# A token mixer of two attentions and a router on Trainium2: the small jobs in another order, and two lists of row numbers for the scatters

## The reference

```python
h = layernorm(x) * (1 + ca) + sa
# linear attention, 16 heads of 16
qf, kf = elu(q) + 1, elu(k) + 1
out = (qf @ (kf.T @ v)) / (qf . sum(kf) + 1e-6)
x = x + ga * (out @ wo.T + bo)
h = layernorm(x) * (1 + cb) + sb
# softmax attention, 16 query heads of 16, 4 heads of keys and values
src = h + softmax(q @ k.T / 4) @ v @ ow + ob
src = rmsnorm(src) * norm1_w
# router: the two best of 8 experts a row; a capacity for each expert
probs = sigmoid(src @ gate_w); sel, w = top2(probs)
ranks = number of earlier rows of the same expert
padded[sel * capacity + ranks] = src        # if ranks < capacity
out = experts(padded) gathered, weighed and summed
x = x + gb * rmsnorm(src + out) * norm2_w
```

## Time and profile before

| | us |
|---|---|
| median of 3 runs | 3377.61 |
| lowest and highest | 3371.54 and 3377.68 |
| the profiled execution, its own time | 3384.39 |
| its span, first to last instruction | 3382.7 |
| the mixer's steps in it, first to last weighing (L3188) | 1366.4 to 2716.3 |

### The profile page before, as it was taken

The page is one execution under the profiler, slowest core; times in us unless marked ns, Lnnn a source line. Parts: engine busy times, 40 slices in busy tenths (PEclk is TensorE's granted clock), DMA queues, the critical chain, the costliest instruction groups (busy, mean ns, idle before and its releaser), DMA issues. The chain is left out here.

```text
span 3382.7 us, 58016 instructions
## 1 busy us (share of the span) xinstructions
PE 3135.4 (93%) x18353; PEld 1927.6 (57%) x18353; DVE 2082.6 (62%) x5622; ACT 1663.4 (49%) x3743; POOL 1118.9 (33%) x1508
## 2 busy tenths in 40 slices
PE   7899999999989976999999999999998859999997
PEld 3667767677665653344444444444443348888882
DVE  7777777777772233677777777777777632222226
ACT  3565565655641113666666666666665611111116
POOL 2132232322342123334444444444443322222224
PEclk9999999999999988999999999999999979999998
DMA  8110110101125841112222222222222137777758
GB/s 288 5 73 36 57 51 36 72 36 66 42 88 200 303 169 29 54 54 72 74 73 73 74 73 73 68 73 72 71 73 72 51 99 238 230 235 238 225 169 298
DMA packets 266210, 370.48 MB, mean 110 GB/s; under 512 B 41615, under 2 KB 201579, under 8 KB 263904
## 3 DMA queue, kind: packets, MB, share of 16 engines
q1 hardware_dynamic: 250592, 329.82, 30.2%
q0 software_dynamic: 14832, 34.57, 2.8%
q10 hardware_dynamic: 544, 3.15, 0.2%
HBM read 242.38 MB, written 130.39 MB: 110 GB/s over the span
## 5 line engine op out<-in xcount | busy, mean ns | idle before, releaser
L2425 ACT ACTIVATE pT<-psum 128x512 f32<-128x512 f32 x1024 | 599.1, 599 | 363.2 <-PE psum L3176 348.0
L2709 DVE TENSOR_REDUCE negmax<-psum 128x2 f32<-128x1024 f32 x512 | 624.7, 1220 | 213.8 <-PE psum L3146 198.8
L3176 PE MATMUL psum<-q_stack,k_stack 99*128 99x512 bf16 x1024 | 378.8, 383 | 19.0 <-ACT pT L2425 12.0
L3146 PE MATMUL psum<-k_stack,q_stack 96*128 96x512 bf16 x1024 | 308.1, 382 | 53.7 <-DVE negmax L2709 36.4
L944 ACT ACTIVATE probs<-probs,negmax 128x256 f32<-128x256 f32 x512 | 252.8, 495 | 138.6 <-DVE negmax L1036 135.0
L3492 ACT ACTIVATE actT_x<-psum 128x512 f32<-128x512 f32 x142 | 84.8, 597 | 445.0 <-PE psum L3558 445.0
L3522 DVE COPY ye<-psum 128x512 f32<-128x512 f32 x71 | 49.1, 691 | 400.0 <-PE psum L3570 400.0
L3188 PE MATMUL psum<-pT,v_tile 128*32 128x512 f32 x2048 | 274.3, 608 | 1.0 <-ACT pT L2425 1.0
L3480 POOL DMA_INDIRECT chosen_out<-ye,place x142 | 140.0, 986 | 401.1 <-DVE ye L3522 241.1
L3558 PE MATMUL psum<-xT_x,w_x 128*128 128x256 f32 x1136 | 259.3, 382 | 0.0
L3570 PE MATMUL psum<-w_x,actT_x 128*128 128x256 f32 x1136 | 256.6, 379 | 0.0
(11 more groups left out here) (391 smaller groups left out, 5865.4 us busy)
## 6 DMA issues: line engine op xcount, KB each, us to landing
w_x<-in_L_ffn_w_dram SPq DMA_DIRECT2D x142, 512.0 KB
w_e<-in_L_ffn_w_dram SPq DMA_DIRECT2D x46, 1024.0 KB, 7.2
q_stacks<-q_part SPq DMA_DIRECT2D x192, 128.0 KB
q_stack<-q_stacks SPq DMA_DIRECT2D x64, 384.0 KB, 3.5
padded<-w_e SPq DMA_DIRECT2D x32, 645.0 KB, 5.6
xe<-padded SPq DMA_DIRECT2D x71, 258.0 KB
gate_rows<-mods SPq DMA_DIRECT2D x66, 256.0 KB, 3.3
chosen_out<-w_e SPq DMA_DIRECT2D x16, 1024.0 KB, 7.5
```

The costliest lines, as they stand in the source:

```text
L2425: act.activation(pT[:, 4 * (s % 2) + r, :], bank(m, 2 + n % 2), ACT.Exp, scale=float(DHQ) ** -0.5)\
L2709: dve.tensor_reduce(negmax[:, p // 2, h:h + 2], m.psum[:, at:at + 2, :], AX.X, ALU.max, negate=True)\
L3146: mm = pe.matmul(bank(m, at + j), q_stack[0:K_SCORE, h, t * P:(t + 1) * P], k_stack[0:K_SCORE, g, :], start=True, stop=True)
L3176: pe.matmul(bank(m, 2 + n % 2), k_stack[:, g, kc * P:(kc + 1) * P], q_stack[:, REP * g + r, :], start=True, stop=True).then_inc(sT_done, 1)
```

## The change

It changes the order of the jobs in the five `body` functions. PE, DVE and ACT: most jobs move by half a step to two steps. POOL and SP: the queues are turned and in part reordered. Two other edits: `scatter_idx` becomes two lists, one for each parity of the batch, so the wait for the scatters of the batch before moves from DVE's `place` to POOL's first `scatter`; and `store_src` waits for the store of the batch before. Lines 2080 and on carry other numbers afterwards. The cores of the diff, POOL first:

```diff
-        scatter_idx = sb("scatter_idx", [P, NT, TOPK], U32)
+        scatter_idx = sb("scatter_idx", [P, 2, NT, TOPK], U32)
...
             def store_src(b, par):
                 sp.wait_ge(src_ready, b * NT + NT)
+
+                if isinstance(b, int) and b > 0:
+                    sp.wait_ge(src_out, b * 16)
...
                 take_wait(pool, m)
-                pool.indirect_dma_start(padded_dram, bass.IndirectOffsetOnAxis(ap=scatter_idx[:, t, k:k + 1], axis=0),
+                if j == 0:
+
+                    wait_from(pool, scattered, b * (NT * TOPK * 16))
+                    take_wait(pool, m)
+                pool.indirect_dma_start(padded_dram, bass.IndirectOffsetOnAxis(ap=scatter_idx[:, par, t, k:k + 1], axis=0),
...
             def body(b, par, part):
                 if part(1):
-                    last_part(b + 1, 0)
+                    last_part(b + 1, 1)
+                if part(2):
+                    add_bias(b + 2)
+                if part(2):
+                    key_features(b + 2, 1)
+                if part(2):
+                    key_features(b + 2, 0)
...
+                if part(2):
+                    last_part(b + 2, 0)
                 if part(3):
-                    normalise_first(b + 3)
+                    query_features(b + 3, 1)
...
                 step = Steps(dve, place_s, b * PLACE_STEPS, PLACE_STEPS)
                 dve.wait_ge(rank_read, b + 1)
 
-                wait_from(dve, scattered, b * (NT * TOPK * 16))
```

ACT, where `query_exp` of half 1 moves from step 6 to step 2 and that of half 0 stays in step 7, one exponential sooner:

```diff
-                    if s == 6 and part(2):
-                        query_exp(b + 2, 1)
...
+                    if s == 7 and part(2):
+                        query_exp(b + 2, 0)
...
+                    if s == 2 and part(2):
+                        query_exp(b + 2, 1)
```

PE, where `key_values_sum` moves from step 11 to the second half of step 9, and `transpose_hidden` of half 0 to that of half 1:

```diff
-                    if s == 0 and part(2):
-                        transpose_hidden(b + 2, 0)
...
                     if s == 0 and part(2):
+                        transpose_hidden(b + 2, 0)
+                    if s == 0 and part(2):
                         transpose_hidden(b + 2, 1)
...
+                    if s == 9 and part(2):
+                        key_values_sum(b + 2)
...
-                    if s == 11 and part(2):
-                        key_values_sum(b + 2)
```

More of the change, by code:

```diff
@@ L2479, in body @@
                         copy_weighed(b - 1, 3)
+                    if s == 2 and part(0):
+                        copy_max(b, 1)
                     if s == 3 and part(2):
                         key_value_parts(b + 2, 0)
-                    if s == 4 and part(0):
-                        copy_weighed(b, 0)
                     if s == 4 and part(1):
@@ new lines, in body @@
+                    if s == 5 and part(1):
+                        first_part(b + 1, 1)
+                    if s == 6 and part(-1):
+                        copy_o2T(b - 1, 1)
+                    if s == 6 and part(3):
+                        first_seed(b + 3)
+                    if s == 7 and part(2):
+                        key_exp(b + 2, 1)
+                    if s == 8 and part(0):
+                        copy_weighed(b, 1)
+                    if s == 9 and part(-1):
+                        rms_seed(b - 1)
@@ new lines, in body @@
+                    if s == 12 and part(0):
+                        copy_weighed(b, 2)
+                    if s == 13 and part(-1):
+                        logits_exp(b - 1)
+                    if s == 13 and part(2):
+                        copy_o1T(b + 2, 0)
+                    if part(0):
+                        exps(b, s, 3)
+                    if s == 0 and part(2):
+                        query_parts(b + 2, 0)
+                    if s == 1 and part(2):
+                        query_parts(b + 2, 1)
@@ L2536, in body @@
+                    if s == 4 and part(1):
+                        first_part(b + 1, 0)
+                    if s == 4 and part(2):
+                        key_exp(b + 2, 0)
+                    if s == 5 and part(1):
+                        values_part(b + 1)
                     if s == 7 and part(2):
                         key_value_parts(b + 2, 2)
-                    if s == 8 and part(0):
-                        copy_weighed(b, 1)
-                    if s == 9 and part(2):
-                        key_exp(b + 2, 3)
@@ L2542, in body @@
-                    if s == 12 and part(-1):
-                        copy_srcT(b - 1, 1)
-                    if s == 13 and part(-1):
-                        logits_exp(b - 1)
+                    if s == 8 and part(2):
+                        key_value_parts(b + 2, 3)
             body(-3, 1, lambda k: k == 3)
@@ L2935, in body @@
                         residual_stats(b - 1, 1)
-                    if s == 9 and part(-1):
-                        rms_newton(b - 1)
+                    if s == 9 and part(3):
+                        first_newton(b + 3)
+                    if s == 10 and part(2):
+                        key_values_sum(b + 2)
+                    if s == 10 and part(-1):
+                        rms_newton(b - 1)
+                    if s == 11 and part(-1):
+                        scale_src(b - 1, 1 - par, 1)
@@ new lines, in body @@
+                    if s == 12 and part(2):
+                        divide(b + 2, 1)
+                    if s == 13 and part(2):
+                        divide(b + 2, 3)
+                    if s == 14 and part(-1):
+                        choose_top(b - 1)
+                    if s == 15 and part(2):
+                        gate(b + 2, 0)
+                    maxima(b, 2 * s + 1, part)
+                    if s == 0 and part(1):
+                        second_stats(b + 1, 1)
+                    if s == 0 and part(0):
+                        values(b, par)
@@ new lines, in body @@
+                    if s == 0 and part(1):
+                        second_variance(b + 1, 1 - par)
+                    if s == 1 and part(-1):
+                        normalise(b - 1, 1)
+                    if s == 1 and part(0):
+                        cut_max(b, 1)
+                    if s == 2 and part(1):
+                        second_norm(b + 1, 1 - par, 0)
+                    if s == 4 and part(3):
+                        first_stats(b + 3, 1)
+                    if s == 5 and part(3):
+                        first_variance(b + 3)
@@ L2938, in body @@
+                    if s == 5 and part(0):
+                        cut_max(b, 2)
+                    if s == 5 and part(1):
+                        part_remainder(b + 1, 1)
+                    if s == 6 and part(-2):
+                        place(b - 2, par)
+                    if s == 7 and part(-1):
+                        residual(b - 1, 1)
+                    if s == 8 and part(-1):
+                        mean_square(b - 1)
                     if s == 9 and part(0):
                         cut_max(b, 3)
-                    if s == 10 and part(3):
-                        first_newton(b + 3)
```

305 lines of the change are left out of this document (117 added, 188 removed).

## The result

The changed kernel takes 3433.02 us (median of 4 runs, 3427.99 to 3447.49), the kernel before on the same chip 3376.15 (4 runs, 3371.54 to 3377.68). The ratio is 1.0178, with a 95% interval of 1.0143 to 1.0213: by the medians the change costs 57 us. The forecast was 3456 us, 79 more than before, with a range of 3392 to 3492.

A forecast was written before the change was run, and what follows sets the result against it. PE, busy 93%, bounds the kernel. Order -31, transposes +12, POOL's queue +88, clock +7 and ahead of the loop +3 sum to +79 us on the profiled 3384.39: 3463, or 3456 against the median; range 3392 to 3492.

The forecast's parts named there:

- main mechanism: POOL's wait counts both query-feature exponentials, so key features come late and PE's key-value product waits 3.8 us a body.
- the release at W7 + 1.3: When ACT's late query-feature exponential frees POOL's queue: 1.3 us after the weighing matmul of step 7 (W7).
- the second wait: PE at step 10's first pair waits for the next key stacks; with the key-feature wait 6.3 us a body, +88 us.
- the clock: PE's granted clock falls in most bodies, mostly inside the wait for stacks: 0.5 us a body, +7 us.
- rival 1: Only the key features are late, the stacks land with them: 3.8 us a body, not 6.3; 3421 us; chance 0.13.
- rival 2: Worse: clock falls behind each wait (+1.4 us a body), two loads slow the first (+0.9); 3488 us; chance 0.18.
- Evenness: The new order on PE, DVE and ACT fills thin half steps, cutting PE's waits 2.2 us a body, -31 us.
- Two transposes: Hidden-row transposes back to back in step 0 share a bank; the second waits 0.87 us for ACT, +12 us.
- Ahead of the loop: Before the loop, batch 0's keys' part on POOL stands behind one query feature job: +3 us (0 to 6).
- The body: Sign expected in the changed profile: a body lasts 92 to 93 us.
- The double list frees nothing that was waited for: Second scatter index list is memory alone; the wait moved from DVE's placing to POOL's scatter 0 counts 0.
- Rival 3: Faster: POOL released in time or steps 7 to 9 longer, only evenness (-31) and transposes (+12) count; 3362 us; chance 0.12.

The follow-up runs named there:

- experiment 1: Changed kernel with the two halves of the query features exchanged on ACT and POOL; 3397.58 us, ratio 1.0073 to the kernel before.
- experiment 8: Kernel before with scatters 1 to 6 moved on POOL behind the last key feature; 3371.24 us, ratio 0.9999.
- experiment 3: Changed kernel with four extra, useless matmuls on PE ahead of its wait for key features; 3413.47 us, ratio 1.0121 to the kernel before.
- experiment 5: Changed kernel with query feature halves exchanged, hidden-row transposes apart again and POOL's normalise_first moved back; 3362.14 us, ratio 0.9977 to the kernel before.
- experiment 9: Kernel before with only the two transposes of the hidden rows put directly behind each other; 3386.59 us, ratio 1.0045.
- experiment 4: Changed kernel with one list of row numbers and the wait for scatters back in DVE's place; 3540.21 us, ratio 1.0501 to the kernel before.
- experiment 10: Kernel of experiment 5 with DVE's place in step 4 instead of step 6; 3359.22 us, ratio 0.9962 to the kernel before.

## Why the prediction was right, and where it was wrong

**Direction and main mechanism: right.** POOL's queue behaves as worked out, to 0.2 us in both of its points, and L3065 waits 3.5 us in each of ten bodies where 3.8 were forecast (38.5 us over all 13, 3.0 on the mean). Exchanging the halves alone takes the wait away (experiment 1). One step of the working has no reason given for it: the release at W7 + 1.3 takes 0.60 off twice and names one exponential. Measured, ACT's exponential ends at W7 + 1.2, so the place was right; with 0.60 taken off once, all of POOL's points would have been 0.6 later. That the whole came within 23 us is in part luck: two terms were wrong in opposite directions, the second wait by 28 us too much and the clock by 9 to 13 too little.

**The step that failed: the second wait.** The prediction put the stacks at W7 + 18.6, from 9.5 us between POOL's keys' part and the load's issue plus 3.9 to land, and let this wait swallow the first, at 6.3 us a body. Measured, the issue comes 7.3 us behind the keys' part (1940.49 to 1947.83) and the pair at W7 + 16.6 (1951.80) does not wait. The wait for stacks is 0.5 us a body in place of 2.5, thus 28 us too much over 14 bodies. The prediction's own sign of being wrong, that k_stack never holds PE, nearly came true: in the loop it does so three times, for 1.2 us in all. The term that was mis-sized is the landing of six stores: 3.1 us for 4.4, and experiment 8 shows that it was the scatters beside them that the old row held. The other 0.9 us of the 2.2 is the choice of the body: the 9.5 was read where SP waited 5.3 us for the stores, the longest of all, against a mean of 4.4, which rival 1 had noted. The landing was carried over as a property of the stores, though the change moved what was in flight beside them. Rival 1 had just this case; its 3421, with the clock at its measured 16 to 20 us instead of 7, is 3430 to 3434, and 3433 was measured. The Trainium skill, page "DMA: Bandwidth & Descriptors", section "Anatomy of one DMA", gives 2.0 us for the fixed cost of one DMA on GpSimd's path. The six stores here are issued by SP, so it is a neighbour's figure, and neither row comes down to it, though the sign in which it differed from the old row was right.

**The clock: mis-sized.** +7 was taken; experiment 3 gives 16 to 20, the ledger 1.2 to 1.4 us a body, about the figure of rival 2. The prediction reasoned that the fall would lie inside the second wait. There was none, so the slow matmuls lay on the path. The Trainium skill, page "TensorE: Matmul & The Clock Gate", section "HAM oscillation", describes bursts that start at half clock behind each wait; the rows agree, a granted clock of 0.50 to 0.60 in the four microseconds behind each wait of 3.5 us.

**Evenness: right in size, not durable.** -31 was taken, 2.2 us a body. The ledger has -2.7 a body, and -1.9 against the trace of experiment 8. But once the long wait is gone (experiment 5), PE's waits are 28 us where they were 38 to 47.5, -0.7 to -1.4 a body, and its time is 9 us under the kernel before. That part of the evenness in the changed kernel was DVE catching up while PE stood still would explain it, and was not shown by itself. So the price of the wait and the gain of the order can't be read off one ledger as if they were independent.

**Two transposes: right,** +12 forecast, 12.4 us of waits, 12.7 measured by themselves (experiment 9). **Ahead of the loop,** +3 was taken and the first weighing comes 1.0 us later. **The body** was to last 92 to 93 us and lasts 90.15.

**"The double list frees nothing that was waited for": wrong in the new order.** It was read from the trace of before, in which DVE never waits there. But the forecast itself had POOL stand still with the last scatter queued behind the wait, and had to ask who waits for that: DVE's `place`, 10 us a body (experiment 4). The sum did not suffer, as both edits came together.

**Missed altogether: DVE held by POOL's runs.** Rival 3 said that if the key features came in time the kernel would take 3362. Experiment 1 makes them come in time and takes 3397.58. Neither rival nor sum had DVE's small operations held by POOL's runs; only with two more jobs moved is 3362.14 reached (experiment 5), and that it meets rival 3's number is chance, as the transposes are apart in it.

What stays open: in experiment 1 a body takes 1.7 us more than in the trace of before (88.7 for 87.0) at the same waits (3.6 and 3.5 us a body). All of it is PE's busy time, 84.9 us a body for 83.2. In experiment 5, with the granted clock at 1.00, it is 83.3, so most of the 1.7 goes with the clock that falls in some bodies (below); no run changes the clock alone there. Nor was the wait of `store_src` tried; the profile shows none on it.

## What to carry to other kernels

A semaphore that counts jobs makes the early job wait for the late one when the producer makes them in another order than the consumer asks: check producer order against consumer order for each counted wait, and list what is queued behind it. A wait or landing time read from the old trace holds for the old neighbours; when the change moves what lies beside it (scatters beside stores, POOL's runs beside DVE's small operations), bound it again. And before a new order is judged, repair its one bad wait and look at the timeline once more: the first repair uncovers what the wait had hidden.

## What the hardware showed beyond that

**POOL's runs hold DVE's small operations in SBUF.** `ranked` (two inputs, 64 columns) takes 0.21 us free and 2.81 beside back-to-back POOL operations of about 0.7 us each; the copy of 16 columns 0.18 to 1.77. Moved away from POOL's run it is back at 0.21 (experiment 10), and the copy falls when POOL's run is moved (experiment 5). The reductions from PSUM never last longer than 1.23 us in the stretch. The Trainium skill, page "SBUF — State Buffer", section "SBUF: two separate sides", says that VectorE and GpSimd share one pair of ports under an exclusive lock, that the pair is kept for the whole instruction and the other engine blocks. The traces agree that it blocks, and show more: 2.6 us is over three of POOL's operations, so DVE was passed over where one of them ended and the next began. It was not held to the end of the run either, as it ended 0.6 us before that. What decides its turn was not shown.

**Stores land later beside scatters:** 4.4 against 3.1 us for the same six (experiment 8).

**The clock does not fall by the length of one wait alone.** In the earlier trace rows 2.75 us of waiting left it at full. In the changed kernel it fell behind 2.67 us of waiting for the stacks that ended at 1502.06, with 0.94 us of waiting for DVE some 4.5 us before:

```profile
1502.00:1506.00 4.00, 3.94 (x18) 1.46 (x19) 2.16 (x8) 1.67 (x3) 0.99 (x2) 0.64 0.10 33
```

In the first experiment's kernel it fell behind 1.38 us of waiting in one body, and in the next, behind 1.44 us, it did not:

```profile
1845.14 0.38 PE L3170 MATMUL psum<-ident_bf,max_part 128*12 128x128 bf16 x4 [1.38 <-issue]
...
1934.41 0.38 PE L3170 MATMUL psum<-ident_bf,max_part 128*12 128x128 bf16 x4 [1.44 <-DVE max_part L2732]
```

```profile
1844.00:1852.00 8.00, 6.45 (x24) 3.04 (x28) 6.74 (x17) 2.14 (x4) 3.31 (x6) 0.79 0.01 3
1932.00:1940.00 8.00, 6.17 (x32) 2.28 (x36) 7.83 (x17) 2.92 (x7) 4.54 (x8) 1.00 0.05 18
```

The two stretches hold much the same waits, and the granted clock (third number from the end) is 0.79 in one and 1.00 in the other.
